# Two expert phases: one variance for both normalisations, features turned in the outputs' banks, and the last four pairs finished stage by stage

## The reference, cut to what matters

```python
# x, down, ffn(x): [32, 56, 128]
up   = einsum('eud,bsd->bseu', w_up, x) + b_up             # 8 experts, 512 wide
down = einsum('edu,bseu->bsed', w_down, gelu(up)) + b_down
ffn  = the two chosen experts' down, weighted
x = layernorm(x + ffn(x))            # (x - mean) / sqrt(var + 1e-5), over 128 features
# the next block begins with a second layernorm of this x, with a gain and a bias:
h = layernorm(x) * ln_g + ln_b
```

## Time and profile before

| | |
|---|---|
| three runs, median (lowest to highest) | 1886.55 us (1885.76 to 1887.1) |
| the profiled execution's own time | 1884.88 us |
| its span in the trace | 1883.0 us |
| busy: PE, DVE, ACT, POOL | 89%, 82%, 68%, 49% of the span |
| first mixture's expert phase, from the first work to the last | 347.3 to 550.9 us |
| second mixture's expert phase | 1725.9 us to the end |
| mean granted clock of TensorE over the span | 0.96 of full speed |

### The profile page before, as it was taken

The page is one execution under the profiler, slowest core; times in us unless marked ns, Lnnn a source line. Parts: engine busy times, 40 slices in busy tenths (PEclk is TensorE's granted clock), DMA queues, the critical chain, the costliest instruction groups (busy, mean ns, idle before and its releaser), DMA issues. The chain is left out here.

```text
span 1883.0 us, 34675 instructions
## 1 busy us (share of the span) xinstructions
PE 1667.1 (89%) x10425; PEld 1009.4 (54%) x10425; DVE 1549.9 (82%) x2885; ACT 1275.3 (68%) x2106; POOL 925.5 (49%) x723
## 2 busy tenths in 40 slices
PE   4987996889957899999999999999999999994997
PEld 2654665777733344554554554454455455454886
DVE  2765785877758999999999999999999999975887
ACT  2442332877735887887888788788788888864554
POOL 3640111363335766565665656656567465421333
PEclk9997998799978999999999999999999999997998
DMA  5203884311100898988899898898888889973231
GB/s 190 95 0 127 306 332 173 85 42 45 45 34 17 180 197 174 199 182 179 190 183 190 183 190 187 178 195 182 179 199 179 188 183 185 182 135 122 47 79 29
DMA packets 632266, 281.85 MB, mean 150 GB/s; under 512 B 601852, under 2 KB 606236, under 8 KB 631452
## 3 DMA queue, kind: packets, MB, share of 16 engines
q1 hardware_dynamic: 632204, 281.10, 64.2%
HBM read 129.02 MB, written 1.05 MB: 69 GB/s over the span
## 5 line engine op out<-in xcount | busy, mean ns | idle before, releaser
L2237 DVE SCALAR_TENSOR_TENSOR xa_h<-xa_psum,xa_rinv,xa_h 128x500 f16<-128x500 f32 x672 | 452.8, 730 | 1.0 <-ACT xa_h L2445 0.7
L2445 ACT ACTIVATE xa_h<-xa_psum,xa_rinv 128x1000 f16<-128x1000 f32 x448 | 371.5, 883 | 51.8 <-DVE xa_rinv L2228 51.5
L2429 ACT ACTIVATE xa_psum<-xa_psum,xa_bias,unscale_s 128x1500 f32<-128x1500 f32 x224 | 353.2, 1577 | 7.4
L2073 PE MATMUL xa_psum<-xa_c_hi,xa_q_hi 128*128 128x500 f16 x672 | 257.4, 383 | 54.5 <-DVE xa_h L2237 50.1
L2217 DVE TENSOR_REDUCE xa_psum<-xa_psum 128x1 f32<-128x1000 f32 x224 | 269.3, 1202 | 14.2 <-PE xa_psum L2075 13.4
L2098 PE MATMUL xa_psum<-xa_prT,xa_n_hi 128*128 128x512 f16 (+1 forms) x768 | 270.8, 353 | 3.6 <-issue 1.6
L2100 PE MATMUL xa_psum<-xa_prT,xa_n_lo 128*128 128x512 f16 (+1 forms) x768 | 270.6, 352 | 0.0
L2099 PE MATMUL xa_psum<-xa_prT,xa_n_hi 128*128 128x512 f16 (+1 forms) x768 | 270.6, 352 | 0.0
L2074 PE MATMUL xa_psum<-xa_c_lo,xa_q_hi 128*128 128x500 f16 x672 | 252.7, 376 | 0.0
L2075 PE MATMUL xa_psum<-xa_c_hi,xa_q_lo 128*128 128x500 f16 x672 | 252.4, 376 | 0.0
L1939 POOL TENSOR_SCALAR xa_ctxT<-xa_ctxT,scales 128x1500 f32<-128x1500 f32 x31 | 126.3, 4073 | 166.4 <-DMA xa_ctxT<-in_ctxT 166.4
(11 more groups left out here) (328 smaller groups left out, 3630.4 us busy)
## 6 DMA issues: line engine op xcount, KB each, us to landing
ctxN<-in_ctxP SPq DMA_DIRECT2D x16, 1536.0 KB, 9.5
xa_ctxP<-in_ctxP SPq DMA_DIRECT2D x32, 768.0 KB, 4.3
ctxT<-in_ctxT SPq DMA_DIRECT2D x16, 1500.0 KB, 6.4
xa_ctxT<-in_ctxT SPq DMA_DIRECT2D x32, 750.0 KB, 4.7
moe_spread<-weight_rows SPq DMA_DIRECT2D x16, 1024.0 KB, 8.4
xa_prT<-xa_h SPq DMA_TRANSPOSE x192, 5.5
up<-in_F_up SPq DMA_DIRECT2D x1, 2048.0 KB, 7.7
down<-in_F_down SPq DMA_DIRECT2D x1, 2048.0 KB, 11.8
```

The source lines that it names most:

```text
L2073: nc.tensor.matmul(out, qh, c_hi[:, b, a:z], start=True, stop=False)
L2237: nc.vector.scalar_tensor_tensor(low, psum[:, bank + a:bank + z, 0:W], rinv[:, s % 2, :], high, ALU.mult, ALU.subtract).then_inc(h2_ready, 1)
L2429: nc.scalar.activation(psum[:, bank:bank + 3, 0:W], psum[:, bank:bank + 3, 0:W], ACT.Exp, bias=bias[:, s % 2, :], scale=k.unscale_s[:, :], ...
L2445: nc.scalar.activation(h[:, H_SLOT[s], 0, a * W:z * W].rearrange("p (a c) -> p a c", c=W), psum[:, bank + a:bank + z, 0:W], ACT.Identity, ...
```

## The change: what it does

Three things change, all in `expert_phase`.

The variance of the second normalisation is no longer measured. With v the variance of `r`, the normalised values have variance v / (v + EPS), and both normalisations together are a division by sqrt(v (1 + EPS) + EPS^2). `inner_root` on POOL computes that from the first `bn_aggr`, and DVE makes `xn2` straight from `r`. `xn2` is now made at the start of expert `p+2`, and `xn`, which only `x_tok` needs, later in that expert.

The features' transpose goes to columns 128 to 255 of the bank that holds the output's transpose of the pair behind it (6 or 7), one expert earlier (`e = p+2`). Before it PE now waits until DVE has read that bank (`r_ready`), and before the output's transpose until ACT has stored the features (`feat_stored`). `project` no longer waits for `feat_stored`.

The drain is written out per engine (`drain`): each stage is done for all four pairs before the next, in four different banks, and POOL's work is done in one instruction for four pairs.

```diff
-            for e in range(1, CK + 3):
-                for at in range(-1, 3):
-                    tail(CHUNKS - 1, e, at, after=True)
+            drain(CHUNKS - 1)
...
+            def inner_root(i, p):                                    # POOL
+                pool.wait_ge(t.mean_var_ready, n(i, p))
+                pool.sem_inc(rooting, 1)
+                pool.tensor_scalar(t.var_eps2[:, p, :], t.mean_var[:, p, 1:2], 1.0 + EPS, EPS * EPS, ALU.mult, ALU.add)\
+                    .then_inc(t.var_eps2_ready, 1)
+                pool.wait_ge(t.var_eps2_ready, n(i, p))
+                pool.sem_inc(rooting, 1)
+                pool.wait_ge(t.xn2_ready, b(i, p))
+                pool.tensor_tensor(t.rstd2[:, p, :], t.var_eps2[:, p, :], k.minus_half[:, :], ALU.pow).then_inc(t.rstd2_ready, 1)
...
                 if 0 <= e - 1 < CK:                                  # POOL, tail
+                    if inner:
+                        inner_root(i, e - 1)
                     t.pool_rstd(pool, i, e - 1)
                 if 0 <= e - 2 < CK:
-                    if inner:
-                        t.pool_inner_rstd(pool, i, e - 2)
                     if not final:
                         t.pool_store(pool, i, e - 2)
...
+            def drain(i):                                            # POOL
+                pool.wait_ge(t.mean_var_ready, n(i, CK - 1))
+                if inner:
+                    pool.tensor_scalar(t.var_eps2[:, :, :], t.mean_var[:, :, 1:2], 1.0 + EPS, EPS * EPS, ALU.mult, ALU.add)\
+                        .then_inc(t.var_eps2_ready, CK)
+                pool.tensor_tensor(t.var_eps[:, :, :], t.mean_var[:, :, 1:2],
+                                   k.eps[:, :].unsqueeze(1).to_broadcast([128, CK, 1]), ALU.add).then_inc(t.var_eps_ready, CK)
...
+                    pool.tensor_tensor(t.rstd2[:, :, :], t.var_eps2[:, :, :], power, ALU.pow).then_inc(t.rstd2_ready, CK)
...
+                pool.tensor_tensor(t.rstd[:, :, :], t.var_eps[:, :, :], power, ALU.pow).then_inc(t.rstd_ready, CK)
+                if not final:
+                    pool.wait_ge(t.xn_ready, n(i, CK - 1))
+                    pool.tensor_copy(k.x_tok[:, i * CK:(i + 1) * CK, :], t.xn[:, :, :]).then_inc(t.tok_stored, CK)
...
                 def project(e):                                      # PE
                     pe.wait_ge(part_ready, slot(i, e))
-                    if not first and not final and 0 <= e - 3:
-                        pe.wait_ge(t.feat_stored, last(i, min(e - 2, CK), CK))
...
                     pe.wait_ge(t.r_ready, this(i, e - 2, CK) if e >= 3 else last(i, CK, CK))
+                    if not final:
+                        pe.wait_ge(t.feat_stored, this(i, e - 3, CK) if e >= 4 else last(i, CK, CK))
                     nc.tensor.transpose(psum[:, 6 + e % 2, 0:128], mixed[:, 2 * (e - 1):2 * e, :], k.ident[:, :])\
                         .then_inc(y_ready, 1)
-                if at == 2 and 0 <= e - 3 < CK and not final:
-                    ...
-                    t.tensor_transpose(pe, i, e - 3, psum[:, 4 + e % 2, 128:256])
+                if at == 2 and 0 <= e - 2 < CK and not final:
+                    pe.wait_ge(t.r_ready, this(i, min(e, CK), CK))
+                    if e >= 4:
+                        pe.wait_ge(t.feat_stored, this(i, e - 3, CK))
+                    t.tensor_transpose(pe, i, e - 2, psum[:, 6 + e % 2, 128:256])
+            def drain(i):                                            # PE
+                for p in range(CK):
+                    nc.tensor.transpose(psum[:, p, 0:128], mixed[:, 2 * p:2 * p + 2, :], k.ident[:, :]).then_inc(y_ready, 1)
+                if not final:
+                    for p in range(CK):
+                        t.tensor_transpose(pe, i, p, psum[:, p, 128:256])
...
+            def drain(i):                                            # DVE: r x4, bn_stats x4, bn_aggr x4,
+                ...                                                  # xn2 x4 (inner), xn x4
...
-                if at == 2 and 0 <= e - 3 < CK and not final:        # ACT
-                    t.scalar_store(act, i, e - 3, psum[:, 4 + e % 2, 128:256])
+                if at == 2 and 0 <= e - 2 < CK and not final:
+                    t.scalar_store(act, i, e - 2, psum[:, 6 + e % 2, 128:256])
```

More of the change, by code:

```diff
@@ L1248, in expert_phase, with run @@
         out_stored, hi_ready, lo_ready = sem("out_stored"), sem("hi_ready"), sem("lo_ready")
+        rooting = sem("rooting")
         block = ctx.enter_context(nc.Block())
-        def run(engine, chunk, tail):
+        def run(engine, chunk, tail, drain):
             chunk(0, lambda e, at: None, first=True)
@@ L1311, in chunk, with tail @@
                         .then_inc(acc_ready, 1)
-            def tail(i, e, at, after=False):
+            def tail(i, e, at):
                 if at != 1:
@@ L1563, in tail @@
                     t.vector_moments(dve, i, p)
+                if inner and at == 1 and 0 <= e - 2 < CK:
+                    t.vector_normalise(dve, i, e - 2)
                 if at != -1:
@@ L1567, in tail @@
                 if 0 <= p < CK:
-                    t.vector_normalise(dve, i, p)
-                    if inner:
-                        t.vector_inner_moments(dve, i, p)
-                p = e - 3
-                if inner and 0 <= p < CK:
-                    t.vector_inner_normalise(dve, i, p)
-            run(dve, chunk, tail)
+                    if inner:
+                        dve.wait_ge(t.rstd2_ready, n(i, p))
+                        dve.wait_ge(t.xnT_ready, b(i, p))
+                        nc.vector.tensor_scalar(t.xn2[:, p, :], t.r[:, p, :], t.mean_var[:, p, 0:1], t.rstd2[:, p, :],
+                                                ALU.subtract, ALU.mult).then_inc(t.xn2_ready, 1)
+                    else:
+                        t.vector_normalise(dve, i, p)
+            def drain(i):
+                for p in range(CK):
+                    dve.wait_ge(y_ready, n(i, p))
+                    nc.vector.tensor_tensor(t.r[:, p:p + 1, :], psum[:, p, 0:128].unsqueeze(1),
+                                            k.x_tok[:, bass.ds(i * CK + p, 1), :], ALU.add).then_inc(t.r_ready, 1)
+                for p in range(CK):
+                    dve.wait_ge(t.r_ready, n(i, p))
+                    nc.vector.bn_stats(t.moments[:, p, :], t.r[:, p, :]).then_inc(t.moments_ready, 1)
+                for p in range(CK):
+                    dve.wait_ge(t.moments_ready, n(i, p))
+                    nc.vector.bn_aggr(t.mean_var[:, p, :], t.moments[:, p, :]).then_inc(t.mean_var_ready, 1)
+                if inner:
+                    dve.wait_ge(t.rstd2_ready, n(i, CK - 1))
+                    dve.wait_ge(t.xnT_ready, b(i, CK - 1))
+                    for p in range(CK):
+                        nc.vector.tensor_scalar(t.xn2[:, p, :], t.r[:, p, :], t.mean_var[:, p, 0:1], t.rstd2[:, p, :],
+                                                ALU.subtract, ALU.mult).then_inc(t.xn2_ready, 1)
+                for p in range(CK):
+                    t.vector_normalise(dve, i, p)
+            run(dve, chunk, tail, drain)
         @block.scalar
@@ L1629, in chunk, with tail, drain @@
                         x_high(i + 1)
-            def tail(i, e, at, after=False):
-                if at == 2 and 0 <= e - 3 < CK and not final:
-                    t.scalar_store(act, i, e - 3, psum[:, 4 + e % 2, 128:256])
-            run(act, chunk, tail)
+            def tail(i, e, at):
+                if at == 2 and 0 <= e - 2 < CK and not final:
+                    t.scalar_store(act, i, e - 2, psum[:, 6 + e % 2, 128:256])
+            def drain(i):
+                if not final:
+                    for p in range(CK):
+                        t.scalar_store(act, i, p, psum[:, p, 128:256])
+            run(act, chunk, tail, drain)
 def expert_phase0(k):
```

20 lines of the change are left out of this document (11 added, 9 removed).

## The result

The kernel after takes 1868.57 us (median of four runs, 1867.0 to 1872.36) beside 1886.37 of the kernel before: a ratio of 0.9918, interval 0.9906 to 0.993. The forecast of 1876.7 and its range from 1872 to 1882 lie above it. The direction was right; the size forecast was too small.

The account below looks back on a forecast made before the run. PE was taken to bound the chunks with a tail, the latency chain the drains. Terms -7.1 - 3.8 - 0.9 + 2.0 = -9.8 us on 1884.88 gave 1875.1; with 1.67 for the median, 1876.7, range 1872 to 1882.

Parts of the forecast that it names:

- First drain: Drain of the first expert phase, four pairs stage by stage: 7.1 us less, bounds 5.2 and 7.5.
- Last drain: Drain of the last expert phase, at the kernel's end: 3.8 us less, bounds 3.0 and 4.1.
- What the inner normalisation loses: DVE's dropped second moments and moved `xn2`: worth nothing by itself in the chunk loop, DVE having time to spare.
- The banks, in the loop: PE's waits in the chunk loop: old ones go, nine for `r` come; -0.9 us, between -1.5 and 0.0.
- The clock: PE in the chunk loop: idling at the new waits lowers its clock once per chunk; +2.0 us, bounds 0 and 9.6.
- The base: Whole kernel: the median of the runs was taken as 1.67 us above the profiled execution's 1884.88.
- The rival without a fall of the clock: Chunk loop: the new waits never lower PE's clock; -11.8 us, 1874.7, down to 1873.4; chance 0.32.

Follow-up runs that it names:

- the two repeats: The kernel after, unchanged, measured twice more: 1869.66 us (ratio 0.9933), and 1870.66 us (ratio 0.9928) on another chip.

## Why the prediction missed

The forecast was 9.8 us of gain, the change is worth 14.3. Step by step:

- **First drain, 7.1 forecast, 7.8 measured.** Right in its chain and in what is late last, but 0.3 beyond its bound of 7.5: 0.3 of the difference is POOL's copy, 0.35 the first three stages on DVE.
- **Last drain, 3.8 and 4.1.** Right, at the upper bound.
- **What the inner normalisation loses, 0 in the loop; 2.7 measured.** This step failed. "DVE has 12 us to spare per chunk, so this is worth nothing by itself there" took the share of busy time for slack. DVE had time to spare, but `xn2` was late for its one consumer: nine of twelve transposes followed it by 0.15 us or less, and cost PE up to 1.1 us each. The prediction had the row that tells it, 829 ns beside 346 and a collision with POOL's addition, and gave it no price; it counted the 0.87 of the third chunk as coming "once per chunk", where the fourth has 0.45 and the second none listed. The run with one variance and old banks has the 2.7 us.
- **The banks, in the loop, -0.9 (-1.5 to 0.0) together with the wait for `xn2`.** That nine waits cost about what the shorter ones cost was right: the loop is as long with new banks (133.9) as with old ones (133.7). The waits are 0.9 to 1.4 us against a forecast of 1.3 to 1.7; `hidden(2)` to `project(6)` is 32.25 in the third chunk, at the low end of 32.2 to 32.7, and 31.8 and 31.9 in the second and fourth, where the first step is 6.2 and 6.4 us instead of 6.7. The measured sum, -2.5, is outside the bounds.
- **The clock, +2.0; 0 measured.** This failed too. The granted clock was 1.00 from the first of the nine waits to the last, and the same in the two repeats, 27 waits. The forecast interpolated between a wait of 0.87 without a fall and one of 1.99 with one, and took 1.5; the waits were 1.2. The run with a later `r` shows that the price is real, 1.3 and 1.5 us, but its two falls stand behind waits of 1.9 and 2.6, and six of the eight waits of 1.6 to 2.7 had none. By the rule of the Trainium skill (TensorE: Matmul & The Clock Gate, "A second HAM failure mode: psum-queue depth-cycling") falls were to be expected at such waits, for which it names no length. At 1.2 us the traces do not agree, and in the run with a later `r` they agree behind two of nine waits.
- **The base.** The 1.67 us that were added to come from the profiled execution to the median was chance of three runs: over 67 executions the kernel before has a mean of 1884.3, not 1886.55. That is 2.2 of the 6.5 us between the forecast and 1870.2, the mean of the kernel after; 1.6 (loop), 2.0 (clock) and 1.0 (drains) are the rest, 0.3 more than is needed. The first median of after, 1868.57, lies another 1.6 below that mean. The range counted only terms of the change, and not that either kernel by itself moves by several us.

The rival without a fall of the clock, 1874.7 and down to 1873.4, had the clock right, but it too gave the variance nothing in the loop. The prediction priced the right new wait, and read that it comes from the place of `r` behind four `low`; that the place could be changed, for 12.5 us, it did not ask.

What stays open: why a half-speed stretch comes in one execution of a phase and not in another, why the untouched stretch between the drains varies by 4.5 us, which part of the one variance gives the 2.7 us, and what two engines in one bank would do without the wait for `r`; that was not tried, since it would be a race.

## What to carry to other kernels

An engine with idle time in a stretch can still be late for each of its consumers: sum the stretches between the same two instructions of the waiting engine over all repeats, and compare them with the shortest one, rather than trust busy shares or the listed waits. An instruction that takes more than twice as long as its twin of the same shape is a place to look: ask who waits for it. When a change puts in a wait for a small result, look at once what that result is queued behind on its engine; here one line moved ahead of two others turned a neutral change of banks into 12 us. And profile the unchanged kernel twice before pricing tenths of a per cent, to know which parts of the time move by themselves.

## What the runs showed of the hardware

- Phases with the same instructions differ from execution to execution: in 13 profiles the first `y` comes between 396.2 and 401.6 us, with 55 us at half clock ahead of it in the earliest and 62 to 69 in the two latest, and 67 executions of one kernel lie between 1880.8 and 1891.1.
- 27 waits of PE of 0.9 to 1.4 us were followed by no fall of the clock; of nine of 1.1 to 2.7 us two were (behind 1.9 and 2.6), at 1.3 and 1.5 us each.
- DVE's `xn2` (128x128) took 0.91 to 1.27 us beside POOL's addition of 128x448 and 0.33 to 0.35 elsewhere.
- POOL's power took 0.55 us on one column (two of them per pair in a drain) and 1.02 on four; its copy of 128x512, 0.61 in the idle drain where the next phase had 0.93.
